# Gated cross-attention and quantised FFN: the opening rebuilt around natural-layout splits and DMA transposes

## The reference

```python
x = x + tanh(g_xattn[0]) * (fq(layernorm(x)) @ fq(ctx))      # fq: round to 0..255 with scale and zero point
x = x + tanh(g_ffn[0]) * ffn(layernorm(x))

# ffn(x), weights w_gate, w_up [2752, 1024], w_down [1024, 2752]
A, g = quant_act(x)                  # g = max(|x|) / (448*6) over ALL elements; x/g in fp8 by blocks of 16,
                                     # the last 128 columns quantised twice (the value and its error)
Wg, Wu = quant_w(w_gate), quant_w(w_up)          # int4 by blocks of 16
h = silu(A @ Wg.T * g) * (A @ Wu.T * g)
Am, gm = quant_act(h)
y = Am @ quant_w(w_down).T * gm
```

## Time and profile before

| | us |
|---|---|
| median of 3 runs | 898.81 |
| the profiled execution | 897.22 |
| its span | 895.4 |
| TensorE busy | 760.2 (85%) |
| VectorE busy | 647.7 (72%) |
| POOL busy | 296.6 (33%) |
| ScalarE busy | 287.9 (32%) |

### The profile page before, as it was taken

One profiled execution on the slowest core, in us unless ns is written; L12 is line 12 of the kernel. 1 busy time (PEld: TensorE's weight loads), 2 busy tenths in 40 slices (PEclk: granted clock), 3 DMA queues, 4 the chain that ended last, 5 costly groups with the idle time before them and its releaser, 6 DMA issues.

```text
span 895.4 us, 10681 instructions
## 1 busy us (share of the span) xinstructions
PE 760.2 (85%) x3638; PEld 357.9 (40%) x3643; DVE 647.7 (72%) x1027; ACT 287.9 (32%) x364; POOL 296.6 (33%) x165
## 2 busy tenths in 40 slices
PE   0689100579999999999999999999789989999998
PEld 0234100445554444444444444444334434444443
DVE  6999789988766575767576676642489999989820
ACT  2964420331234343434353433431022221121100
POOL 1001135745316574858575756640000000000000
PEclk9999555589999999999999999999989999999999
DMA  7734300110034979788888979770515467654420
GB/s 297 223 103 153 117 23 0 48 57 22 27 114 105 233 171 225 158 205 182 206 198 189 209 172 229 169 160 23 197 36 117 123 159 171 136 141 133 110 58 23
DMA packets 188836, 121.41 MB, mean 136 GB/s; under 512 B 161792, under 2 KB 173056, under 8 KB 187776
## 3 DMA queue, kind: packets, MB, share of 16 engines
q1 hardware_dynamic: 188800, 120.96, 54.0%
HBM read 61.88 MB, written 19.66 MB: 91 GB/s over the span
## 4 chain that ended last, share of the span: by engine, by line
PE 71%; DVE 21%; ACT 2%; issue 2%; DMA 2%; POOL 1%; SPq 1%; DVEq 0%; ACTq 0%
PE acc L986 46%; PE acc L1037 23%; DVE bst L1104 2%; PE tb L920 2%; DVE big L1283 1%; DVE wbuf L1209 1%; DVE h_in L1282 1%; DVE big L1134 1%; DVE h_in L1227 1%; DVE w_max L1197 1%; DMA mid<-wbuf 1%; DVE h_in L1281 1%; DVE mid L1215 1%; DVE mid L1181 1%; DVE wbuf L1179 1%
## 5 line engine op out<-in xcount | busy, mean ns | idle before, releaser
L986 PE MATMUL acc<-mid 128*128 128x512 f16 (+1 forms) x2112 | 447.7, 375 | 0.0
L986 PEld LDWEIGHTS acc<-mid 128*128 128x128 f16 x2112 | 207.1, 98 | 238.8 <-issue 1.3
L1037 PE MATMUL acc<-big,mid 128*128 128x512 f16 x1056 | 231.8, 382 | 9.8 <-DMA mid<-wbuf 8.6
L585 POOL TENSOR_TENSOR wbuf<-wbuf,w_inv 128x1024 f32<-128x1024 f32 (+1 forms) x68 | 127.9, 1887 | 159.3 <-DVE w_inv L1203 159.3
L1037 PEld LDWEIGHTS acc<-big,mid 128*128 128x128 f16 x1056 | 103.7, 98 | 137.4 <-issue 9.1
L622 POOL TENSOR_TENSOR h_in<-wbuf,h_in 128x1024 f16<-128x1024 f32 (+1 forms) x56 | 114.5, 2044 | 86.7 <-ACT h_in L808 86.6
L1354 DVE SCALAR_TENSOR_TENSOR h_out<-acc,gs,silu 128x256 f32<-128x256 f32 (+1 forms) x88 | 41.4, 471 | 116.1 <-ACT silu L766 99.4
L711 ACT ACTIVATE wbuf<-wbuf 128x1024 f32<-128x1024 f32 (+1 forms) x68 | 69.1, 1017 | 93.2 <-POOL wbuf L585 92.5
L1197 DVE TENSOR_REDUCE tb<-wbuf 128x64 f32<-128x1024 f32 (+1 forms) x56 | 65.4, 1168 | 40.1 <-DMA wbuf<-in_L_ffn_w_gate_dram 21.8
L808 ACT ACTIVATE h_in<-wbuf 128x1024 f16<-128x1024 f32 (+1 forms) x56 | 57.0, 1019 | 114.7 <-DVE wbuf L1209 114.7
L766 ACT ACTIVATE silu<-acc,gs 128x256 f32<-128x256 f32 (+1 forms) x88 | 40.1, 457 | 91.6 <-PE acc L986 88.0
(11 more groups left out here) (153 smaller groups left out, 600.4 us busy)
## 6 DMA issues: line engine op xcount, KB each, us to landing
h_in<-h_d SPq DMA_DIRECT2D x8, 1376.0 KB, 7.1
wbuf<-in_L_ffn_w_gate_dram SPq DMA_DIRECT2D x21, 512.0 KB, 4.1
wbuf<-in_L_ffn_w_up_dram SPq DMA_DIRECT2D x21, 512.0 KB, 4.1
h_d<-h_out SPq DMA_DIRECT2D x80, 128.0 KB, 3.4
wbuf<-in_L_ffn_w_down_dram SPq DMA_DIRECT2D x16, 512.0 KB, 4.4
wbuf<-in_ctx_dram SPq DMA_DIRECT2D x12, 512.0 KB, 4.3
big<-in_x_dram SPq DMA_DIRECT2D x8, 512.0 KB, 6.5
x_d<-big SPq DMA_DIRECT2D x8, 512.0 KB, 3.9
```

Source lines behind the costliest of these rows:

```text
L585: pool.tensor_tensor(w, w, spread(w_inv[0:rows, b, 0:cols // BLK]), ALU.mult).then_inc(w_scaled, 1)
L986: last = pe.matmul(acc[m % 4][:, 0:cols], left[:, k, s * P:(s + 1) * P], ring[:, slot, right, k, 0:cols], start=(k == 0 and left is a_hi a ...
L1037: last = pe.matmul(acc[2 * i + hf][:], amT[:, i, k // DH, left, k % DH, :], right[:, k, hf * MW:(hf + 1) * MW], start=(k == 0 and left == ...
```

## The change

The diff touches the opening only (stages 1 to 3). In its parts:

- *Loads.* SP issues x0, x1, the parameters, x2, x3 and ctx 0 to 3 before the rest; ctx tiles go to buffers in xn_all, so wbuf is free for weight pieces from the start. The P pieces are three full ones instead of four.
- *Layernorm of x* is done for tiles 0 to 3 and for 4 to 7 apart. ScalarE's affine steps become Relu (clip at 0). VectorE's first step clips at 255 and adds the magic number. For ctx the second step goes to POOL (`shift_ctx`); for x it stays.
- *Row term.* `make_x1` no longer waits for `base`; the row sums come after the last attend, and `base` runs after `norm`, before the x1 stores.
- *Splits in natural layout.* All W, X and P pieces and all A tiles are split before they are turned: hi by ScalarE (`hi_open`, `hi_a`), lo by POOL (`lo_open`, `lo_a`), and turned by DMA transposes. The float32 transposes on TensorE and the `lo_part`, `hi_part` of the opening go.
- *A quantisation* is that of the down stage: `start_a`, ScalarE's floor, `end_a`, with reciprocals (`a_coef_unbound`) taken before g is known. POOL does nothing for it but the lo part.
- *Order.* OPENING becomes a flat list of products; X pieces are turned after product P7.

```diff
-OPENING = (
-    ((("A", 0), ("A", 1), ("W", 0), ("W", 1)), (("P", 0), ("P", 1))),
...
+OPENING = (("P", 0), ("P", 1), ("P", 2), ("P", 3), ("U", 0), ("U", 1), ("U", 2), ("U", 3),
+           ("P", 4), ("P", 5), ("U", 4), ("U", 5), ("P", 6), ("P", 7), ("U", 6), ("U", 7))
+P_PIECES = 3
 # SP
+            for t in range(2):
+                load_x(t)
             for i, p in enumerate((s1, z1, s2, z2, g_xattn, g_ffn)):
...
+            for t in range(2, 4):
+                load_x(t)
+            for c in range(4):
+                load_ctx(c)
...
+            def turn_open(n, slot, at):
+                b = buf(n)
+                sp.wait_ge(nat_lo, n + 1)
+                sp.dma_start_transpose(ring[:, slot, :, :, at * P:(at + 1) * P].rearrange("p v k n -> p (v k) n"),
+                                       nat[b][:, 0:2 * H]).then_inc(piece_turned[b], 16)
+            def turn_a(t):
+                sp.wait_ge(nat_a_lo, t + 1)
+                for v, a in enumerate((a_hi, a_lo)):
+                    sp.dma_start_transpose(a[:, :, t * P:(t + 1) * P], nat_a[:, t % 2, v, :]).then_inc(a_across[t % 2], 16)
...
+            for t in range(NT):
+                store_x1(t)
+            turn_a(0)
+            turn_a(1)
+            turn_w(0)
+            turn_w(1)
...
+            sp.wait_ge(mm_done, OPEN_TILE[("P", NT - 1)] + 1)
+            for j in range(4):
+                turn_x(j)
+                store_open(OPENING[11 + j])
 # POOL
+            def shift_ctx(c):
+                pool.wait_ge(ctx_clip, c + 1)
+                pool.tensor_scalar(ctxq[:, c, :], ctx_buf[c % CTX_BUFS], nmrz[:, 1:2], 1.0, ALU.add, ALU.mult).then_inc(ctx_quant, 1)
-            def a_times_coef(t):
-            def a_times_scale(t):
+            def lo_open(n):
+                b = buf(n)
+                pool.wait_ge(nat_hi, n + 1)
+                pool.tensor_tensor(nat[b][:, H:2 * H], wbuf[:, b, :], nat[b][:, 0:H], ALU.subtract).then_inc(nat_lo, 1)
+            def lo_a(t):
+                pool.wait_ge(nat_a_hi, t + 1)
+                pool.tensor_tensor(nat_a[:, t % 2, 1, :], xn_all[:, t, :], nat_a[:, t % 2, 0, :], ALU.subtract).then_inc(nat_a_lo, 1)
 # VectorE
+            def clip_ctx(c):
+                w = ctx_buf[c % CTX_BUFS]
+                dve.wait_ge(ctx_affine, c + 1)
+                dve.tensor_scalar(w, w, 255.0, MAGIC, ALU.min, ALU.add).then_inc(ctx_clip, 1)
...
+            def start_a(t):
+                v, mg = xn_all[:, t, :], mga[:, t % 2, :]
+                dve.wait_ge(ro_ready, t + 1)
+                step(dve.scalar_tensor_tensor(out=blocks(v), in0=spread(a_coef[:, t, :]), scalar=gs[:, 6:7], in1=blocks(v),
+                                              op0=ALU.min, op1=ALU.mult))
+                dve.tensor_scalar(mg.bitcast(I32), v.bitcast(I32), 0x7F800000, 0x00400000, ALU.bitwise_and, ALU.bitwise_or)\
+                    .then_inc(a_magic, 1)
+            def end_a(t):
+                v, mg = xn_all[:, t, :], mga[:, t % 2, :]
+                dve.wait_ge(a_floor, t + 1)
+                step(dve.scalar_tensor_tensor(out=v, in0=mg, scalar=MAGIC_FLOOR, in1=v, op0=ALU.add, op1=ALU.add))
+                step(dve.scalar_tensor_tensor(out=v, in0=mg, scalar=MAGIC_FLOOR, in1=v, op0=ALU.add, op1=ALU.subtract))
+                return dve.tensor_tensor(blocks(v), blocks(v), spread(a_scale[:, t, :]), ALU.mult)
...
+            start_a(0)
+            start_a(1)
+            a_scales()
+            end_a(0)
+            step(end_a(1))
+            fold_outliers(0)
+            a_coef_unbound(slice(4, NT), step)
+            front_open(3)
+            front_open(4)
+            start_a(2)
+            back_open(3)
+            back_open(4)
+            front_open(5)
+            front_open(6)
+            start_a(3)
+            end_a(2)
+            step(end_a(3))
+            fold_outliers(2)
...
```

More of the change, by code:

```diff
@@ L618, in lo_nat @@
+            lo_open(3)
+            lo_open(4)
+            scale(5, 2)
+            scale(6, 3)
+            lo_a(2)
+            lo_a(3)
+            lo_open(5)
+            lo_open(6)
+            scale(7, 0)
+            scale(8, 1)
+            lo_a(4)
+            lo_a(5)
+            lo_open(7)
+            lo_open(8)
+            scale(9, 2)
+            scale(10, 3)
+            lo_a(6)
+            lo_a(7)
+            lo_open(9)
+            lo_open(10)
             def lo_nat(u, s):
@@ L815, in unit @@
                     if s < UNIT_PIECES:
-                        hi_nat(u, s, first)
+                        hi_nat(u, s)
                     if s < 6:
@@ new lines, in _ @@
+            clip_ctx(9)
+            col_lo(0)
+            quantise_x(4)
+            clip_ctx(10)
+            quantise_x(5)
+            clip_ctx(11)
+            make_x1(0)
+            quantise_x(6)
+            clip_ctx(12)
+            quantise_x(7)
+            clip_ctx(13)
+            make_x1(1)
+            clip_ctx(14)
+            clip_ctx(15)
+            make_x1(2)
+            col_lo(1)
+            step(make_x1(3))
+            aggregate(slice(0, 4))
+            front_open(0)
@@ new lines, in _ @@
+            layernorm(3, slice(0, 4))
+            make_x1(4)
+            front_open(1)
+            make_x1(5)
+            back_open(0)
+            max_a(0)
+            make_x1(6)
+            front_open(2)
+            max_a(1)
+            back_open(1)
+            dve.wait_ge(x_affine, NT)
+            step(make_x1(7))
+            aggregate(slice(4, NT))
+            max_a(2)
+            layernorm(4, slice(4, NT))
+            step(max_a(3))
+            back_open(2)
+            a_coef_unbound(slice(0, 4), step)
@@ L1414, in _ @@
+            front_open(10)
+            start_a(6)
+            start_a(7)
+            h_open(OPENING[6])
+            end_a(6)
+            h_open(OPENING[7])
+            step(end_a(7))
+            h_open(OPENING[8])
+            fold_outliers(6)
+            back_open(9)
+            back_open(10)
+            h_open(OPENING[9])
+            h_open(OPENING[10])
+            front(PIECE_LOOP, 0, 16 * (loads_before(0, 0) + 1), looped=True)
+            for m in OPENING[11:]:
                 h_open(m)
```

816 lines of the change are left out of this document (409 added, 407 removed).

## The result

| | before | after |
|---|---|---|
| median of the runs, us | 898.87 (896.29 to 899.72, 6 runs) | 893.1 (891.79 to 893.78, 6 runs) |
| profiled execution, its span | 897.22, 895.4 | 893.12, 891.3 |
| loop's first product starts | 268.7 | 262.8 |

What follows compares the result with a forecast made beforehand. VectorE, then TensorE, was taken to bound the opening, TensorE the loop. Loop start 114.3 + 116.9 + 9 + 9.9 + 14 = 264.1, 4.6 earlier; 897.2 less 4.6 is 892.6, plus 1.6 gives 894.2 us; range 888 to 900.

Steps and rivals of the forecast that it cites:

- g: The global maximum in the opening, first read by ScalarE; forecast at 114.3 us, 8.7 earlier than 123.0.
- fold 6: The last fold on VectorE's chain in the opening; forecast to end 116.9 us after g.
- P0: First opening product on TensorE; forecast near 140 us, 35 before 174.9, as cover and not gain.
- stall ahead of the loop: TensorE's wait for the X turns behind U6 and U7; forecast as a new stall of 3.7 us.
- The frame: Whole forecast: when the loop starts, plus 626.7 us from there to the span's end, kept as before.
- Stage 1: Opening up to g; first piece's reduction forecast at 71 us instead of about 73.5, with 11 of waits.
- Stage 2: VectorE's chain from g to the last fold: 94.4 us of steps plus 22 of turns taken with POOL.
- The way to the loop: From fold 6 to the loop: 9 us to P6, 9.9 for P6 and P7, 14 for the X turns.
- The constant: From the loop's start to the span's end: 626.7 us kept; wrong if it moves by over 2.
- (a): Rival on VectorE and POOL: fewer collisions, shift about 0.75 (-5), 10 instead of 22 lost (-12); 877 us; chance 0.24.
- (b): Rival on POOL's shift: a two-input kind of cost, 2.13 or more, +11 and +3; 908 us; chance 0.25.
- (c): Rival on DMA: X and A turns queue, 4.3 apart, stall grows by 3.6; 898 us, no change; chance 0.13.

Runs made afterwards that it cites:

- e1: The changed kernel with P0 held until the fifth piece's low part is written; 893.44 us.
- e2: The changed kernel with the fourth X piece turned before product P7 is done, three behind it; 889.52 us.
- e3: The changed kernel with the second ctx step (the shift) back on VectorE and none on POOL; 895.74 us.
- e4: The changed kernel with POOL's low parts written for 16 of 1024 columns only, the rest left out of the result; 880.0 us.
- e5: The changed kernel with the block scales of pieces 0 to 6 in PSUM instead of SBUF; 890.48 us.
- e8: The changed kernel with the edits of e2, e5, e6 and e7 together; 884.97 us.
- e7: The changed kernel with the high part of each A pair turned once rounded, not waiting for the low part; 889.72 us.
- e6: The changed kernel with fronts, scalings and roundings of the third and fourth X piece (9 and 10) moved behind the last fold; 889.36 us.
- e9: The changed kernel with the edits of e2, e5 and e7, fronts 9 and 10 staying ahead of the last fold; 884.22 us.
- e10: The changed kernel with all four edits of e8, but piece 7 is the X piece turned early, ahead of the four loads; 880.53 us.

## Why the prediction was right

| step | predicted | measured |
|---|---|---|
| first quantised A tile | 19.2 | 20.15 |
| one shift on POOL | 1.2 | 1.21 mean (1.12 in most, 1.50 in 4) |
| waits it brings to VectorE | 11 | 6.6, and 3.1 more idle for ScalarE |
| first piece's reduction | 71 | 70.6 |
| g | 114.3 | 113.2 |
| waits of VectorE for POOL, g to fold 6 | 22 | 18.5 |
| fold 6 ends, from g | 116.9 | 117.7 |
| P0 | 140 | 138.1 |
| fold 6 to P6 | 9 | 8.0 |
| P6, P7 and U6, U7 | 9.9 + 10.3 | 20.6 |
| stall ahead of the loop | 3.7 | 3.28 |
| loop starts | 264.1 | 262.8 |
| from there to the end | 626.7 | 628.5 |
| median less profiled execution | 1.6 | 0.0 |

*The sum.* The loop's start was 1.3 early, the stretch behind it 1.8 long, and the 1.6 that I had added because the median before lay above the profiled execution was nothing after: -1.3 + 1.8 - 1.6 = -1.1. Nothing that I can show ties the last two together, and that they nearly cancel is luck. So is a part of the 264.1: my terms to the fold add up to 94.4 + 22 = 116.4, and I wrote 116.9.

*The frame* held: the time is the loop's start plus a stretch that the change leaves alone (it is within 3 us the same in all kernels, see under the constant). The early products were cover and not gain (e1), the stall was a full term (e2).

*Stage 1* came out right as a total (70.6, where I had 71) from two sizes that were off. I gave the waits 11 us. On VectorE's steps they are 6.6, since they fell on 9 instructions (one L1234, four L1236, one L1225, two L1208, the cast) and cost 0.73 each, where I had counted 12 at some 0.9; but VectorE, with less to do, waits 3.1 longer for ScalarE, a term I had left out. 11 against 9.7. e3 measures the whole move: 2.6 us. From there to g it was 42.6, where I had 43.3.

*Stage 2*: 18.5 us of waits, from three groups of the trace: L1477 16.6 less 8 at 1.24 (6.7), L1479 13.8 less 8 at 0.69 (8.3), L1272 4.5 less 4 at 0.23 (3.6; forecast as part of the fronts only). e4 took the differences' share away, 10.7 us, and 8.1 us of the chain went. What is left was thus 99 where I had 94.4. Some 3.4 of the 4.6 are waits of h tiles for silu and for a store, a term that I did not have. A price too high for the collisions and none for these waits offset each other, which is luck.

*The way to the loop* was 1.0 shorter between fold and P6, and 0.4 in the stall. The X turns were issued 3.0 apart and landed 4.3 after the last issue, against 3.1 and 4.7 from the earlier trace rows. I had taken the 3.1 from SP's issue and a store. The transfers alone would keep the turns as far apart. From 251 to 261 us the DMA engines are busy throughout (shares of 0.93 to 1.16 in stretches of 2 us) at 186 to 223 GB/s. A turn of 512 KB and a store of 128 KB between two turns make, at the 215 GB/s that is the mean to 259 us, an estimate of 3.05 us: the distance that was measured. Which of the two sets it no run shows. The Trainium skill (Advanced Engine Details and Errata, section X-Bar Transpose) has transposes by DMA as fast as regular ones, at 350 to 400 GB/s. In landing this trace agrees, 4.3 us for a turn and 4.3 for a load of 512 KB. In rate it does not: 354 and 422 GB/s in the two stretches from 243 to 247 us, behind the four loads, and 205 to 223 in those of the turns. By the estimate from that page the stall would not be there; it is 3.28.

*The constant* was off by 1.8, near the 2 that I had named as my limit. From the loop's start to the transpose of h's maximum (at 643.73 before, 639.50 after) it took 375.0 before and 376.7 after; 376.7 again in e3 and e5 and 376.4 in e8, and 375.0 in the other seven. These rows are that transpose before and after, and then the last 792 products of the down stage, after and in e7:

```profile
643.73 0.29 PE L869 MATMUL tb<-ident,gmx 128*128 128x128 f32 x1 [1.88 <-DVE gmx L1456]
639.50 0.29 PE L1014 MATMUL tb<-ident,gmx 128*128 128x128 f32 x1 [1.88 <-DVE gmx L1616]
...
714.69 172.75 PE L1148 MATMUL acc<-big,mid 128*128 128x512 f16 x792 [4.54 <-DMA mid<-wbuf]
...
711.81 171.10 PE L1148 MATMUL acc<-big,mid 128*128 128x512 f16 x792 [2.78 <-DMA mid<-wbuf]
```

The windows at the loop's start say what differs: granted clock 0.70 in the third of the stretches shown first, lower than 1.00 in e3, e5 and e8 too, and 1.00 in the seven. The stalls ahead were 3.28, 3.28, 3.31 and 4.67 in the first, and 0.32 to 3.45 in the second: the gap's length alone does not decide. I had priced the low clock for P6 and P7 and not here; with it the same stall costs 3.3 or 5.0. What decides it stays open. The down stage has a second place of the kind, ahead of its last 792 products. They take 172.7 to 172.8 before and in the changed kernel, e1, e2, e5, e6 and e8, and 171.1 in e3, e4, e7, e9 and e10. The granted clock right behind the stall is 0.50 in the changed kernel and 1.00 in e7. The stalls are 2.7 to 4.6 in the first group and 2.5 to 3.2 in the second, so again the length does not decide. The stretch from the loop's start to the end of the span is therefore no constant: it runs from 625.9 (e4, e9) to 629.0 (e8).

*The rivals.* (a) 877, fewer collisions: they were nearly as many as I had said, 18.5 of 22. e4 shows that with 10.7 of them gone the time is 880, so the price was rightly placed and the case did not occur. (b) 908: the shift is no two-input kind of cost, 1.12 alone. (c) 898: turns 3.0 apart, not 4.3. The DMA engines were busy all through, as this rival has it, but the distance was close to the forecast's.

## What to carry to other kernels

When a step is moved to an engine that takes turns with the one it leaves, price it as the step less the waits it brings, on every step of the other engine down to those over 4 columns: here 12 us moved, 2.6 won. Look for the chain first and call everything that starts earlier off it a cushion; then ask what the chain's last part waits for, because there edits of order and place alone (a turn of one piece, two fronts, a scale in PSUM) were worth 12.6 us between medians, 1.3% by the ratios, against the rebuilt opening's own 5.8 and 0.6%. And before adding up edits that each pay, name the piece, the buffer and the place in a queue on which each rests: e8 started its loop 2.4 us behind e10 (4.4 in the medians, on two chips), and what differs is the piece that is turned early and its place ahead of the loads. Last, look at what takes the place of a collision that you remove: in e6 the same steps met another instruction of POOL, and in e4 a store.

## What the runs showed of the hardware

- A VectorE step over 4 columns (0.16 us) took 0.90 and 1.78 beside a POOL instruction, another (0.17 alone) 2.10; one over 64 columns in SBUF took up to 2.14, and 0.23 with its operands in PSUM beside the same POOL work.
- The turn-taking goes both ways: POOL's 1.93 became 2.81 and its shift's 1.12 became 1.50 behind a VectorE step.
- TensorE came back from a stall of 3.2 to 3.5 us at a clock of 1.00 in four profiled executions (e1, e4, e6, e7), and in three (changed kernel, e3, e5) at one that fell to 0.50 within 1.5 us of the loop's start, which cost 1.7 us. In the down stage the same 1.7 followed stalls of 2.7 us (e1) and not of 3.2 (e3).
- While 512 KB transposes followed each other, the DMA engines were busy all the time at 205 to 223 GB/s; behind four 512 KB loads they moved 354 and 422.
